# Attention and FP8 feed-forward on one core: a re-ordered prelude, batch 1's rotary products on another engine, and the weights' scale in steps a slot apart

## The reference

```python
xn = layernorm(x)
Q, K, V = xn @ W_q.T, xn @ W_k.T, xn @ W_v.T        # split into 16 heads of 16
Qr, Kr = rope(Q, cos, sin), rope(K, cos, sin)       # pairs (x0, x1) -> (c*x0 - s*x1, s*x0 + c*x1)
scores = where(causal, -inf, Qr @ Kr.T * 16 ** -0.5)
attn = (softmax(scores) @ V) @ W_o.T
xq, wq = fake_quant_fp8(xn), fake_quant_fp8(weight) # one scale a tensor: 448 / max |t|
out = x + attn + (xq @ wq.T + bias)
```

## Time and profile before

| | |
|---|---|
| median of 3 runs | 444.62 us (443.45 to 444.95) |
| profiled execution, its own time | 446.0 us |
| its span, first to last instruction | 444.0 us |
| mean granted TensorE clock | 0.965 |
| busy: PE, DVE, POOL, ACT | 397.3, 359.3, 282.8, 278.9 us |

### The profile page before, as it was taken

How to read it: one execution, slowest core, us unless ns; L and a number is a source line. 1 busy time by engine, 2 the same in 40 slices (tenths; PEclk the granted TensorE clock), 3 DMA queues, 4 the chain that set the end, 5 groups by cost and what they waited for, 6 DMA issues and landing times.

```text
span 444.0 us, 9396 instructions
## 1 busy us (share of the span) xinstructions
PE 397.3 (89%) x2911; PEld 234.7 (53%) x2911; DVE 359.3 (81%) x1372; ACT 278.9 (63%) x505; POOL 282.8 (64%) x284
## 2 busy tenths in 40 slices
PE   7905778987989999999999999999999999999886
PEld 7504553443645655565656565565555554555435
DVE  1997789999797879988898889888988898779314
ACT  3564758564773777567765766677747766657651
POOL 2575685367576678668767786687866764236670
PEclk9956899997998999999999999999999999999999
DMA  8939425833186047733675257623970497020111
GB/s 265 290 130 230 68 74 135 162 62 120 53 162 145 2 131 203 141 54 120 178 140 90 73 172 157 128 74 118 192 144 21 149 211 144 9 95 2 34 64 47
DMA packets 34049, 53.16 MB, mean 120 GB/s; under 512 B 4496, under 2 KB 30480, under 8 KB 31120
## 3 DMA queue, kind: packets, MB, share of 16 engines
q1 hardware_dynamic: 34000, 52.57, 48.3%
HBM read 35.52 MB, written 16.78 MB: 118 GB/s over the span
## 4 chain that ended last, share of the span: by engine, by line
PE 59%; DVE 17%; ACT 8%; issue 7%; DMA 5%; POOL 3%; SPq 1%; POOLq 0%; DVEq 0%; ACTq 0%
PE o_ps L958 13%; PE st_ps L864 12%; PE s_ps L884 9%; PE m_ps L849 8%; DVE scratch L607 8%; PE m_ps L916 5%; PE m_ps L893 5%; ACT prob L724 4%; DMA xnT<-x_dram 2%; DMA q_st<-shift 1%; PE m_ps L924 1%; DMA qk_parts<-parts 1%; POOL parts L320 1%; DVE stats L533 1%; DVE rowmax L607 1%
## 5 line engine op out<-in xcount | busy, mean ns | idle before, releaser
L607 DVE CUSTOM_DVE_ANT_0 scratch<-s_ps,causal 128x512 bf16<-128x512 f32 (+3 forms) x512 | 220.4, 484 | 36.6 <-PE s_ps L884 36.2
L724 ACT ACTIVATE prob<-st_ps 128x512 f32<-128x512 f32 x320 | 174.6, 600 | 105.4 <-PE st_ps L864 104.1
L465 POOL TENSOR_SCALAR_AFFINE_SELECT prob<-prob 128x512 f32<-128x512 f32 (+1 forms) x160 | 90.4, 569 | 122.5 <-ACT prob L724 121.8
L884 PE MATMUL s_ps<-k_st,q_st 96*128 96x512 bf16 (+3 forms) x512 | 122.9, 303 | 22.9 <-DMA k_st<-qk_parts 14.4
L864 PE MATMUL st_ps<-q_st,k_st 98*128 98x128 bf16 (+3 forms) x512 | 123.2, 304 | 10.2 <-ACT prob L724 6.2
L864 PEld LDWEIGHTS st_ps<-q_st,k_st 98*128 98x128 bf16 x512 | 41.4, 97 | 89.7 <-ACT prob L724 48.0
L958 PE MATMUL o_ps<-prob,v_sb 128*17 128x512 f32 (+3 forms) x1024 | 82.7, 440 | 1.2 <-POOL prob L465 0.7
L884 PEld LDWEIGHTS s_ps<-k_st,q_st 96*128 96x128 bf16 x512 | 49.0, 98 | 48.5 <-DVE rowmax L607 15.9
L607 DVE DVE_READ_ACCUMULATOR2_ANT rowmax<- 128x1 f32 x512 | 41.3, 81 | 0.0
L958 PEld LDWEIGHTS o_ps<-prob,v_sb 128*17 128x17 f32 x1024 | 23.0, 97 | 30.4 <-issue 26.4
L320 POOL TENSOR_TENSOR parts<-rot,parts 128x1024 bf16<-128x1024 f32 (+1 forms) x16 | 32.6, 2042 | 2.6 <-ACT parts L710 2.6
(11 more groups left out here) (121 smaller groups left out, 524.9 us busy)
## 6 DMA issues: line engine op xcount, KB each, us to landing
qk_parts<-parts SPq DMA_DIRECT2D x16, 768.0 KB, 4.2
q_st<-qk_parts SPq DMA_DIRECT2D x15, 384.0 KB, 6.2
k_st<-qk_parts SPq DMA_DIRECT2D x15, 384.0 KB, 6.8
xnT<-x_dram SPq DMA_DIRECT2D x8, 512.0 KB, 8.8
q_st<-qk_parts SPq DMA_DIRECT2D x15, 256.0 KB, 4.9
k_st<-qk_parts SPq DMA_DIRECT2D x15, 256.0 KB, 7.7
x_res<-x_dram SPq DMA_DIRECT2D x7, 512.0 KB, 3.3
out_dram<-x_res SPq DMA_DIRECT2D x7, 512.0 KB, 2.9
```

The source lines that it names most:

```text
L465: eng.affine_select(out=ap, in_=ap, compare_op=ALU.is_ge, fill=0.0, base=0, pattern=pat, channel_multiplier=-1).then_inc(masked, 1)
L607: eng.tensor_tensor_reduce(scratch[:, at % 3, col:col + w], s_ps[at % 3][:, col:col + w], causal[:, T - w:T], 1.0, NEG, ALU.add, ALU.max, ...
L724: eng.activation(prob[u][:, half * T:(half + 1) * T], st_ps[ST_BANK[2 * s + half]][:, :], ACT.Exp, scale=SCALE).then_inc(exp_done, 1)
L884: mm = eng.matmul(bank[:, col:col + (qb + 1) * P], q_st[0:ROWS, n % 2, h, qb * P:(qb + 1) * P], k_st[0:ROWS, n % 2, h, 0:(qb + 1) * P], st ...
```

## The change

Six things, in the order of the program.

1. **Loads.** Batch 1's input is loaded ahead of cos and sin, which have a semaphore of their own. Batch 0's parts go out in six DMAs of 256 KB, each part as soon as it is there (`write_first`), where there were two of 768 KB.
2. **The prelude's order.** On DVE: statistics of batches 0 to 2, batch 0's largest value, its ropes with `remainder` and `low` of w = 0 (on POOL before), then statistics of batches 3 and 4, and of 5 and 6, two together; batch 7's in slot -8. On POOL: the memsets of `k_st` and `v_sb` and the weights' remainders come early, and `invert(3)` waits for DVE's last `low` of batch 0. On ACT: the weights' rounding comes before the first copy. PE gets fewer filling matmuls (`keep_busy`) ahead of the first rows and 46 more between batch 0's projections and its first scores.
3. **Batch 1's ropes.** Its four projections stand in slots -7 to -4; ACT copies each from PSUM to SBUF (into `x_res` and `attn`, not in use yet), and POOL makes the eight products. DVE has none of them.
4. **Batch 1's chain** has slots of its own (EARLY_CHAIN), 1 to 4 slots later than before at most steps; for later batches one read moves from offset -18 to -20.
5. **`largest`** of batches 1 to 7 is in slots 2, 4, ..., 14 (batches 0 to 7 in slots 1, 3, ..., 15 before).
6. **The weights' scale and batch 0's quantisation**: the weights' maximum at slot 15 (16), the second spread and the scale at 19 (18), ACT's products at 21 (19), rounding at 22 and 23 (20, 21); `qv` ... `xq` of batch 0 at 24, 25, 27, 28, 30.

```diff
-SPREAD = [(17, "spread", 0, 0), (18, "spread", 0, 1)]
-TURN_SLOT = {3: -10, 4: -9, 5: -7, 6: -5, 7: -3}
+SPREAD = [(17, "spread", 0, 0), (19, "spread", 0, 1)]
+EARLY = {("qk", 0): -7, ("qk", 1): -6, ("qk", 2): -5, ("qk", 3): -4}
+CHAIN = {("rotate", 0): -29, ("high", 0): -28, ("remainder", 0): -27, ("middle", 0): -26, ("low", 0): -25,
+         ("write", 0): -24, ("rotate", 1): -24, ("high", 1): -23, ("remainder", 1): -22, ("middle", 1): -20,
+         ("low", 1): -19, ("write", 1): -18, ("read", 0, 0): -20, ("read", 0, 1): -16, ("read", 1, 0): -12,
+         ("read", 1, 1): -11}
+EARLY_CHAIN = {("rotate", 0): -5, ("high", 0): -4, ("remainder", 0): -3, ("middle", 0): -2, ("low", 0): -1,
+               ("write", 0): 0, ("rotate", 1): -1, ("high", 1): 1, ("remainder", 1): 2,
+               ("middle", 1): 3, ("low", 1): 4, ("write", 1): 5, ("read", 0, 0): 2,
+               ("read", 0, 1): 7, ("read", 1, 0): 8, ("read", 1, 1): 9}
+TURN_SLOT = {3: -LEAD, 4: -LEAD + 1, 5: -LEAD + 2, 6: -LEAD + 4, 7: -LEAD + 6}
...
-    items = [(max(SLOTS * n + off, -LEAD), order[kind, k], kind, n, k) for (kind, k), off in OFFSETS.items()
-             for n in range(NB) if (kind, n) != ("qk", 0)]
+    items = [(EARLY[kind, k] if (kind, n) == ("qk", 1) else SLOTS * n + off, order[kind, k], kind, n, k)
+             for (kind, k), off in OFFSETS.items() for n in range(NB) if (kind, n) != ("qk", 0)]
...
+def chain_at(slot, *step):
+
+    if slot == EARLY_CHAIN[step]:
+        return 1
+    return batch_at(slot, CHAIN[step], 2)
...
-    first, last, loop = (23, 24, 25, 26, 28), (6, 7, 11, 12, 14), (16, 17, 21, 22, 24)
+    first, last, loop = (24, 25, 27, 28, 30), (6, 7, 11, 12, 14), (16, 17, 21, 22, 24)
...
+        def rope_in(k):
+
+            return (x_res, attn)[k // 2][:, 2 * (k % 2):2 * (k % 2) + 2, :].rearrange("p a d -> p (a d)")
+
+        def rope_places(k):
+            return (prod[:, 0, :], prod[:, 1, :]) if k % 2 == 0 else (prod[:, 3, :], prod[:, 2, :])
...
+            def write_first(w):
+
+
+                for t, (done, out_) in enumerate(((hi_done, early_out), (mid_done, early_out), (low_done, parts_out))):
+                    eng.wait_ge(done[w], 2)
+                    eng.dma_start(qk_dram[0, w].rearrange("t r j h n -> (j h) t r n")[:, t],
+                                  parts[:, w, t]).then_inc(out_[w], 16)
...
-            eng.dma_start(cos_sb[:, :], cos).then_inc(w_qk_in, 16)
-            eng.dma_start(sin_sb[:, :], sin).then_inc(w_qk_in, 16)
-            for n in range(1, NB):
+            load_x(1)
+            eng.dma_start(cos_sb[:, :], cos).then_inc(cos_in, 16)
+            eng.dma_start(sin_sb[:, :], sin).then_inc(cos_in, 16)
+            for n in range(2, NB):
...
+            def rope_of_copy(k):
+
+                eng.wait_ge(rope_copied, k + 1)
+                eng.wait_ge(cos_in, 16 * 2)
+                if k % 2 == 0:
+                    eng.wait_ge(rotated[1 - k // 2], 2 + 2 * (k // 2))
+                a, c = rope_places(k)
+                eng.tensor_tensor(a, rope_in(k), cos_sb[:, :], ALU.mult)
+                eng.tensor_tensor(c, rope_in(k), sin_sb[:, :], ALU.mult).then_inc(roped, 1)
...
-            for n in range(3):
-                invert(n)
-            eng.wait_ge(ln_rstd, 6)
+            eng.wait_ge(consts, 6)
             fill_ones(0)
             eng.wait_ge(consts, 7)
-            remainder(eng, 0, 0)
-            low(eng, 0, 0)
+            invert(0)
+            eng.wait_ge(ln_rstd, 2)
+            fill_ones(1)
+            eng.wait_ge(consts, 8)
+            invert(1)
+            eng.wait_ge(ln_rstd, 4)
             split_weights(0)
+            eng.wait_ge(w_split, 1)
+            invert(2)
+            eng.wait_ge(ln_rstd, 6)
             split_weights(1)
+            eng.wait_ge(w_split, 2)
+            eng.memset(v_sb[:, :, :, :], 1.0).then_inc(consts, 1)
+            eng.wait_ge(consts, 9)
+            eng.wait_ge(low_done[1], 2)
+            invert(3)
+            invert(4)
             split_x(1)
-            for n in range(3, 6):
-                invert(n)
-            eng.memset(v_sb[:, :, :, :], 1.0).then_inc(consts, 1)
-            eng.wait_ge(consts, 8)
+            invert(5)
+            invert(6)
...
-                if slot in (-9, -7):
-                    invert({-9: 6, -7: 7}[slot])
-                if slot == -4:
-                    eng.wait_ge(ln_rstd, 2 * NB)
-                    eng.wait_ge(low_done[0], 4)
-                    fill_ones(1)
-                    eng.wait_ge(consts, 9)
-                for off, step, w in ((-29, rotate, 0), (-27, remainder, 0), (-25, low, 0),
-                                     (-24, rotate, 1), (-22, remainder, 1), (-19, low, 1)):
-                    n = batch_at(slot, off, 1)
+                if slot == -LEAD + 2:
+                    invert(7)
+                for name, step, w in (("rotate", rotate, 0), ("remainder", remainder, 0), ("low", low, 0),
+                                      ("rotate", rotate, 1), ("remainder", remainder, 1), ("low", low, 1)):
+                    n = chain_at(slot, name, w)
                     if n is not None:
                         step(eng, n, w)
-                if slot == 21:
+                for k in [k for _, n, k in shared_at(slot, "qk") if n == 1]:
+                    rope_of_copy(k)
+                if slot == 23:
...
+            def statistics(*batches):
+
+                for n in batches:
+                    eng.wait_ge(x_in[n], 16)
+                    for t in range(NQ):
+                        eng.bn_stats(stats[:, n % 2, t, :], x_of(n)[:, t, :]).then_inc(ln_stat, 1)
+                for n in batches:
+                    eng.wait_ge(ln_stat, NQ * (n + 1))
+                    eng.sem_inc(agg_begun)
+                    for t in range(NQ):
+                        eng.bn_aggr(mv_b[:, n % 2, t, :], stats[:, n % 2, t, :]).then_inc(ln_agg, 1)
+                for n in batches:
+                    p = n % 2
+                    eng.wait_ge(ln_agg, NQ * (n + 1))
+                    wait_past(eng, ln_rstd, 2 * (n - 1))
+                    eng.tensor_scalar(ve[:, p, :], mv_b[:, p, :, 1], EPS, None, ALU.add).then_inc(ln_ve, 1)
+                    eng.tensor_scalar(nmean[:, p, :], mv_b[:, p, :, 0], -1.0, None, ALU.mult).then_inc(ln_ve, 1)
...
-                if s == 16:
+                if s == 15:
...
-                if s == 18:
+                if s == 19:
...
-                if s == 20:
+                if s == 22:
...
-            for n in range(4):
+            for n in range(3):
                 statistics(n)
-            eng.wait_ge(w_qk_in, 16 * 4)
+            largest(0)
+            eng.wait_ge(cos_in, 16 * 2)
             rope(0, 0, first_ps[0])
             rope(0, 1, first_ps[1])
             rotate(eng, 0, 0)
             rope(0, 2, first_ps[2])
+            remainder(eng, 0, 0)
             rope(0, 3, first_ps[3])
             rotate(eng, 0, 1)
+            low(eng, 0, 0)
             remainder(eng, 0, 1)
             low(eng, 0, 1)
-            for n in range(4, NB):
-                statistics(n)
+            statistics(3, 4)
+            statistics(5, 6)
...
+                if slot == -LEAD + 2:
+                    statistics(7)
+                if slot in range(2, 2 * NB, 2):
...
-                for kind, n, k in shared_at(slot, "qk", "o", "fin", "mt"):
+                for kind, n, k in [i for i in shared_at(slot, "qk", "o", "fin", "mt") if i[:2] != ("qk", 1)]:
...
+            def copy_projection(k, bank):
+                eng.wait_ge(full["qk"], 4 + k + 1)
+                eng.copy(rope_in(k), bank[:, :]).then_inc(rope_copied, 1)
...
+            eng.wait_ge(w_qk_in, 16 * 2)
+            for parts_of, raw in zip(w_parts, (wq_sb, wk_sb)):
+                eng.copy(parts_of[:, 0], raw).then_inc(w_high, 1)
             copy_turned(0)
             normalise(1)
             normalise(2)
             high(0, 0)
             copy_turned(1)
             middle(0, 0)
+            copy_turned(2)
             high(0, 1)
             middle(0, 1)
-            for parts_of, raw in zip(w_parts, (wq_sb, wk_sb)):
-                eng.copy(parts_of[:, 0], raw).then_inc(w_high, 1)
             high_x(1)
-            copy_turned(2)
             normalise(3)
+            normalise(4)
...
-                    if n + 1 < NB:
-                        normalise(n + 1)
-                if slot == 19:
+                    if n + 2 < NB:
+                        normalise(n + 2)
+                for k in [k for _, n, k in shared_at(slot, "qk") if n == 1]:
+                    copy_projection(k, shared["qk", 1, k])
+                if slot == 21:
...
-                    eng.wait_ge(w_qk_in, 16 * 4)
+                    eng.wait_ge(w_qk_in, 16 * 2)
...
+                    elif (kind, n) == ("qk", 1):
+                        eng.wait_ge(rope_copied, k + 1)
...
-            keep_busy(26)
+            keep_busy(22)
             turn_rows(0)
-            keep_busy(8)
```

(6 more changed lines are left out.)

51 lines of the change are left out of this document (24 added, 27 removed).

## The result

| kernel | runs | median, us | ratio to before, 95% interval |
|---|---|---|---|
| before | 4 | 444.19 (443.45 to 444.95) | |
| changed | 4 | 448.75 (447.79 to 450.52) | 1.0107 (1.0069 to 1.0146) |
| changed, again, beside the experiments | 6 | 449.35 (448.13 to 451.14) | 1.0117 (1.0094 to 1.0141) |

The change makes the kernel 4.6 to 5.0 us slower, outside the forecast's range. The profiled execution took 448.27 us (span 446.6, clock 0.977), only 2.3 more than that of before.

The account below looks back on a forecast made before the run. PE sets the pace from batch 2 on, at 46.4 us a batch, so about the first 160 us decide. The terms sum to -0.2 us, 446.0 to 445.8 profiled; the median is 1.4 lower, 444.4 us, range 440.8 to 447.8.

Parts of the forecast that it names:

- Up to L: Prelude until DVE ends batch 0's last `low` (L): 1.3 us earlier, near 29.0 us.
- L to E: From DVE's last `low` of batch 0 to the first exponent (E): 1.2 us longer, ending at 64.1 us.
- E to F: From the first exponent to DVE's first maximum for batch 1 in slot 10 (F): 3.1 us longer, through late keys.
- F to G, slots 16 to 21: From DVE's first maximum for batch 1 to its maximum of slot 21 (G): 3.0 us less, in slots 16 to 21.
- Slots 21 to 28: Scale's steps: ACT's products +1.1 us, `qv` waiting for POOL's rounding +0.7, exponent `qe` -0.9; sum +0.9, between 0 and 2.
- Slot 28: Projection at the full clock and DVE no longer late there: -3.0 us, bounds 0 to -3.
- Slot 31: PE waits for POOL's `xq`, made after the bias: +1.9 us, 0.5 to 4 with a fall of the clock.
- Later batches: From batch 2 on, where PE sets the pace at 46.4 us a batch: no change.
- The rival that named a fall of the clock where PE sets the pace: PE's clock falls in slot 10 and again at slot 31: +3 us, 447.4 us; chance 0.16.
- the prediction's own sign of being wrong: First exponent off by over 1.5 us, no DMA wait in slot 10, or clock low where PE sets the pace.

Follow-up runs that it names:

- e4: Changed kernel with batch 1's ropes on DVE again, straight from PSUM, without ACT's copies and POOL's products: 446.72 us, ratio to before 1.0046.
- e2: Changed kernel with the steps to the weights' scale and batch 0's quantisation put back to their slots of before: 447.94 us, ratio to before 1.0079.
- e5: e4 with the steps to batch 1's keys a slot earlier: 443.66 us, ratio to before 0.9974.
- e8: e5 with ACT's products, DVE's exponent and POOL's rounding at slots 20, 21, 22 and xq at 29: 438.94 us, ratio to before 0.9865.
- e9: Kernel before with only the scale's steps moved, to the slots they have in e8: 441.52 us, ratio to before 0.9932.
- e1: Changed kernel with POOL's xq in slot 29, ahead of the bias, instead of slot 30: 447.68 us, ratio to before 1.0076.
- e3: Kernel before with only the scale's steps, batch 0's quantisation and the largest values moved to the change's slots: 446.99 us, ratio to before 1.0047.
- e11: e8 with batch 1's ropes moved back to POOL from ACT's copies: 444.28 us, ratio to before 0.9984.

## Why the prediction was wrong

The forecast was a sum of steps near zero. Below, each with its size in the two profiles of each kernel.

- **Up to L: -1.3.** In the pair of first profiles -2.0, but 1.8 of the 30.25 us of before is the late input that its second profile does not have. Over the four profiles of kernels with the old prelude L lies at 28.4 to 30.3 (mean 29.3), over the ten with the new one at 27.8 to 28.5: -1.1. Right.
- **L to E: +1.2.** 62.78 and 62.40 for E, forecast 64.1; POOL's row (1.24 us from start to start, eight products, gapless) is as described, from a start at 46.87 instead of 48.4. Against 64.13 and 62.57 E moved by -0.8 on average. From L to E it is 0.4 to 0.7 us more than before (34.5), where 1.2 were forecast. That the prelude's gain is given back to POOL is shown by e4 (-4.4).
- **E to F: +3.1.** 23.14 and 23.15 before, 26.69 and 27.88 after: +3.6 and +4.7. Right in mechanism, the wait for the shift rows behind the keys' read included (the read landed at E + 25.2 us, forecast 25.1), and too small by about 1; in the second profile the keys' write took 4.5 us instead of the 3.7 counted.
- **F to G, slots 16 to 21: -3.0.** -2.5 and -1.4 from F to G. Slots 16 to 21, of which the step spoke, take 9.69 and 9.72 us instead of 13.0 (forecast 10.05); slots 10 to 16, said to keep their length of 15.4, take 16.2 and 17.4. In the second profile 1.2 us of that are the fall of the clock in slot 10, which the sum did not have. PE waits for DVE at neither spread. Of the 1.60 us of the 2-column `unscale` 1.4 should have gone, and 0.7 did. POOL's rows beside it, of before and of the changed kernel, and `unscale` itself:

```profile
108.17 2.12 POOL L315 TENSOR_TENSOR rot<-rot,parts 128x1024 f32<-128x1024 f32 x1
```

```profile
111.34 2.13 POOL L341 TENSOR_TENSOR rot<-rot,parts 128x1024 f32<-128x1024 f32 x1
112.60 0.90 DVE L642 TENSOR_SCALAR unscale<-amax_b 128x2 f32<-128x2 f32 x1
```

In both, `unscale` ends 0.03 us after POOL's `remainder` (110.32 and 110.29; 113.50 and 113.47), so its length goes by how much of that is still to come. In e2 it took 0.27 us, and the 2-column instruction after it 2.06, beside the same step of POOL.
- **Slots 21 to 28: +0.9, between 0 and 2.** Measured 15.85 before, 19.37 and 19.47 after: **+3.5. This is the step that failed.** It priced the wait of `qv` for POOL's rounding at 0.7. The other terms came out: 0.9 us more in slot 21 for ACT's products (1.1 forecast), and 0.9 less in slots 23 and 27 (0.9). But `qv` itself (1.15) moved too, from slot 23 to the one place where the cast of 1.03 us already stood ahead of the next exponents. 1.01 + 1.15 is the 2.2 us by which slot 24 grew (4.09 against 1.90). PE then waited 2.42 us, its clock fell, and slot 26 took 4.28 and 4.52 instead of 2.89: the sum had no fall here. e5 has the same wait without the fall, and takes 17.85 for these slots. e8 and e9, without the wait and with ACT's products ahead of slot 21, need 14.74, and slot 24 takes 2.95.
- **Slot 28: -3.0.** 6.87 and 6.91 before, 3.95 and 3.89 after. Right, and e2, with 5.34, bears out that half of it was the clock.
- **Slot 31: +1.9, 0.5 to 4 with a fall of the clock.** The wait is 2.06 us in both profiles, as forecast, and in both the clock fell behind it: 21.51 became 25.14 and 25.13 for slots 31 to 40, +3.6. e1 takes 2.8 of it away. In e3, where the clock stayed up behind the same wait, these slots take 23.80, so 2.3 are the wait's and 1.3 the clock's.
- **Later batches: nothing.** 46.4 us each, but from slot 40 to the end of the span it was 280.8 and 281.0 us, and is 279.8 in both: -1.1, nearly all of it in one slot (last section). The forecast did not have this; without it the total would be off by more.

The measured steps, as means of the two profiles: -0.8 + 4.1 - 1.9 + 3.6 - 3.0 + 3.6 - 1.1, and 0.3 in slots 29 and 30, is +4.8; the spans' means differ by 4.2, since G is on DVE and slot 21's exponent, on ACT, comes 0.6 earlier against it than before. So the step that failed is the wait of `qv` in slot 24, priced at 0.7 us; with `qv` itself it came to 2.2 there and, by way of PE's wait and clock, to 1.4 to 1.6 more in slot 26. The terms from E to G and for slot 31 were too good as well, the last within its own bounds. The rival that named a fall of the clock where PE sets the pace had 0.16 (447.4 forecast). It happened in slot 26 and from slot 31 on in both profiles, as the prediction's own sign of being wrong has it, and in slot 10, its first place, in the second: there the fall costs 1.4 us that the rest does not make up (79.05 us from slot 10 to 40 against 77.66). Of the ten profiles with the new prelude eight have the clock down in slot 10. The Trainium skill (TensorE: Matmul & The Clock Gate, Part 1) lets the gate follow PE's activity; the falls behind waits of 2.42 and 2.06 us agree. But e3 had the same 2.06 us wait in slot 31 and kept its clock behind it, and e5 the same 2.42 us wait in slot 24, so whether a fall follows was not to be had from the wait alone; what decides it stays open.

Profile and median: the profiled execution of before stood 1.8 over its median, that of the changed kernel 0.5 under its own (the second one of the changed kernel 1.0 over). The forecast carried the first excess over as a constant. By the second profile of before most of it came from the arrival of one input, to which the changed kernel seems less exposed (L lies within 0.6 us over ten profiles, within 1.8 over four of the old prelude); that this is so because batch 1's rows are now loaded ahead of cos and sin is only argued, no experiment moved that load alone.

What each part is worth, best arranged around: ropes on POOL +5.3 us (e11 against e8); the new prelude and the chain's slots with ropes on DVE about -3 (0.9865 for e8 against 0.9932 for e9); the scale's steps -3.5 in e9's slots, +2.5 in the change's. Such values hold in their surroundings only: in the change's own arrangement the ropes are worth 2.0 to 2.6 (e4).

## What to carry to other kernels

When a step moves a slot, write down what stands in the new slot between it and the next instruction that the bound engine waits for: a wait, the step and its neighbour add up there, where each was hidden in a slot of its own before. Keep a full slot between an engine's product and an in-order reader that stands ahead of the critical instructions. Where the bound engine is made to wait, allow for a fall of its clock behind the wait: here that added 1.2 to 1.6 us in each of three places. And before work moves from a busy engine to an idle one at twice the price, ask which of the two is the queue there: DVE looked full, but POOL was what the first exponent and the keys waited for.

## What was not expected of the hardware

- Two 4 KB transfers of shift rows, issued behind a read of 768 KB, released PE 4.2 to 6.0 us after the issue of the first, in nine profiles of kernels with the new prelude (in the changed one 83.88 to 88.64); the median landing of six such transfers in e4 from 55 to 95 us is 1.7 us. Since the keys' read lands only half a us ahead of them and PE's first maximum for batch 1 needs it, the late keys set slot 10 as much as the order of issue does; no run changed the order alone.
- The arrival of the second input differed by 1.8 us between two executions of one kernel, and all behind it moved along up to slot 40 (by 1.5).
- Slot 134, in batch 6, took 3.1 to 3.5 us in the four profiles with the old prelude, with a wait of PE for shift rows of 0.8 to 1.2, and 2.2 to 3.0 in the ten with the new one (2.18 in six). The second of the two transfers landed 3.2 to 3.6 us after its issue in the first four, 2.0 to 3.1 in the others. No instruction of this slot was changed; the kernels differ in the transfers that went before, among them one read a batch that stands two slots earlier. That gave the changed kernel about 1 us, and why stays open.
